# Expert weights in eight chunks instead of four, spread over the first tiles of the expert stage

## The reference

```
xn  = layernorm(x)                                     # without scale and shift
out = x + attention(xn) + ffn(xn)

attention: q = rmsnorm(xn @ W_cq), kv = rmsnorm(xn @ W_ckv); 16 heads; a head's scores are the sum of
           a 128-wide part without position and a 64-wide part with rotary position; causal softmax; W_o
ffn:       scores = sigmoid(xn @ gate_w)               # 32 experts
           the 6 largest scores of a token, divided by their sum, are its shares
           routed = sum over its 6 experts e of share * (silu(xn @ wg[e]) * (xn @ wu[e])) @ wd[e]
           shared = silu(xn @ sg) * (xn @ su) @ sd     # one expert of width 192 that all tokens use
```

## Time and profile before

| | us |
|---|---|
| three runs | 1453.88, 1455.01, 1455.03 (median 1455.01) |
| the profiled execution | 1453.54 |
| its span, from the first to the last instruction | 1451.8 |
| TensorE busy in it | 1304.7 (90%) |
| VectorE busy | 936.3 (64%) |
| ScalarE busy | 852.0 (59%) |
| GpSimd busy | 588.0 (40%) |

### The profile page before, as it was taken

The page is one execution under the profiler, slowest core; times in us unless marked ns, Lnnn a source line. Parts: engine busy times, 40 slices in busy tenths (PEclk is TensorE's granted clock), DMA queues, the critical chain, the costliest instruction groups (busy, mean ns, idle before and its releaser), DMA issues. The chain is left out here.

```text
span 1451.8 us, 24463 instructions
## 1 busy us (share of the span) xinstructions
PE 1304.7 (90%) x7385; PEld 965.7 (67%) x7385; DVE 936.3 (64%) x3727; ACT 852.0 (59%) x2294; POOL 588.0 (40%) x607
## 2 busy tenths in 40 slices
PE   4899769999998999759999999998898898998996
PEld 3566446777775777548888888875566665665664
DVE  3587678777776777313564332226888889788784
ACT  1455337677666667326566666656666666666663
POOL 1111027777776667400000000004666566566663
PEclk8999979999999999969999999999999999999998
DMA  9777552323237322286955555542232332332321
GB/s 348 302 258 258 235 200 99 109 81 109 99 113 260 103 91 77 73 260 202 336 176 175 181 177 178 177 137 80 77 106 78 108 105 81 105 103 80 104 79 55
DMA packets 132243, 216.98 MB, mean 149 GB/s; under 512 B 14550, under 2 KB 108438, under 8 KB 126870
## 3 DMA queue, kind: packets, MB, share of 16 engines
q1 hardware_dynamic: 99862, 152.48, 30.9%
q0 software_dynamic: 18432, 50.36, 10.7%
q10 hardware_dynamic: 13824, 12.59, 2.8%
HBM read 103.70 MB, written 111.67 MB: 148 GB/s over the span
## 5 line engine op out<-in xcount | busy, mean ns | idle before, releaser
L1707 ACT ACTIVATE l_prob<-l_prob,l_negmax 128x512 f32<-128x512 f32 (+3 forms) x256 | 142.1, 556 | 153.1 <-DVE l_negmax L1793 153.0
L1062 POOL DMA_INDIRECT sorted_x<-f_xn_row,slot_no x192 | 203.9, 1062 | 49.8 <-issue 49.1
L1218 ACT ACTIVATE f_prob<-f_prob,f_negmax 128x512 f32<-128x512 f32 (+3 forms) x256 | 142.6, 557 | 121.3 <-DVE f_negmax L1291 119.2
L1600 PE MATMUL ps<-l_kt,l_qt 128*128 128x512 f32 (+3 forms) x512 | 176.0, 451 | 39.0 <-DVE l_qt L1771 22.4
L1538 POOL DMA_INDIRECT l_rows<-sorted_y,slot_no x192 | 185.5, 966 | 49.2 <-issue 41.6
L2123 DVE TENSOR_TENSOR act_f<-hidden,ps 128x96 f32<-128x96 f32 x224 | 56.9, 254 | 223.7 <-ACT hidden L2098 223.0
L2060 PE MATMUL ps<-wgu_sb,xt_e 128*128 x896 | 186.1, 331 | 2.0 <-ACT xt_e L2093 2.0
L1291 DVE CUSTOM_DVE_ANT_0 f_prob<-ps,mask_add 128x512 f32<-128x512 f32 (+3 forms) x256 | 121.0, 486 | 86.4 <-issue 85.4
L1121 PE MATMUL ps<-kt_s,f_qt 128*128 128x512 f32 (+3 forms) x512 | 170.2, 447 | 5.0 <-DVE f_qt L1282 4.4
L1793 DVE CUSTOM_DVE_ANT_0 l_prob<-ps,mask_add 128x512 f32<-128x512 f32 (+3 forms) x256 | 121.9, 484 | 70.9 <-issue 69.7
L1566 POOL MEMSET l_one<- 128x1 f32 x1 | 0.1, 99 | 373.3 <-POOLq L1991 373.3
(11 more groups left out here) (202 smaller groups left out, 2955.9 us busy)
## 6 DMA issues: line engine op xcount, KB each, us to landing
sorted_x<-zeros SPq DMA_DIRECT2D x14, 2048.0 KB, 9.0
rows_in<-sorted_x SPq DMA_DIRECT2D x112, 256.0 KB, 2.9
sorted_y<-rows_out SPq DMA_DIRECT2D x112, 256.0 KB, 2.1
wgu_sb<-in_wgu SPq DMA_DIRECT2D x8, 768.0 KB, 14.0
x_in<-in_x SPq DMA_DIRECT2D x8, 512.0 KB, 9.7
xn_dram<-xn SPq DMA_DIRECT2D x8, 512.0 KB, 3.7
base_dram<-x_in SPq DMA_DIRECT2D x8, 512.0 KB, 2.9
nqt_dram<-nqt_out SPq DMA_DIRECT2D x8, 512.0 KB, 3.9
```

Source lines behind the costliest of these rows:

```text
L1062: pool.indirect_dma_start(sorted_x, bass.IndirectOffsetOnAxis(ap=slot_no[:, t, k:k + 1], axis=0), xn_row[buf][:], None).then_inc(scattered ...
L1218: act.activation(prob[:, i, qt, 0:w], prob[:, i, qt, 0:w], ACT.Exp, bias=negmax[:, i, qt:qt + 1], scale=-1.0, accum_out=rowsum[:, g // 2 % ...
L1600: mm = pe.matmul(s_ps[k % 2][:, 0:w], qt[g // 2 % 2][g % 2][:, n * P:w], kt[b - HB][:, 0:w], start=True, stop=True)
L1707: act.activation(prob[:, i, qt, 0:w], prob[:, i, qt, 0:w], ACT.Exp, bias=negmax[:, i, qt:qt + 1], scale=-1.0, accum_out=rowsum[:, g // 2 % ...
```

## The change

The weights come in eight chunks of four experts (three DMAs of 384 KB each). Two of them, as many bytes as chunk 0 had, are loaded in `heads_first`, at the same place. The other six stand in SP's list of the expert stage ahead of pairs 0, 2, 4, 6, 8 and 10. Four pairs of rows instead of three are loaded at the end of `heads_first`; so the load at pair 0 of the stage falls away. The wait for the last store of `heads_first` moves to the second iteration of the stage. As the store may now be under way while chunks arrive, `f_res` is moved out of the room into storage of its own, and `f_lat`, of the same size, takes its place in the room.

```
 class ExpertWeights:
-    CHUNKS = 4
+    CHUNKS = 8
     EACH = NE // CHUNKS
+    EARLY = 2
 ...
-            taken = size // self.CHUNKS
+            taken = self.EARLY * size // self.CHUNKS
 ...
-        for r in range(self.AHEAD - 1):
+        for r in range(self.AHEAD):
             sp.dma_start(self.rows_in[r][:], in_pairs[r]).then_inc(self.in_loaded[r], 16)
 ...
-    res = room_c.sb("f_res", [P, TT, H])
+    res = sb("f_res", [P, TT, H])
 ...
-    lat = sb("f_lat", [P, 2, S])
+    lat = room_c.sb("f_lat", [P, 2, S])
 ...
-            weights.load_chunk(sp, 0, wgu, wd)
+            for n in range(weights.EARLY):
+                weights.load_chunk(sp, n, wgu, wd)
 ...
-            sp.wait_ge(res_stored, 16 * HB + 16)
 ...
             def body(i):
                 for d in range(PAIRS):
+                    if i == 0 and d % 2 == 0 and weights.EARLY + d // 2 < weights.CHUNKS:
+                        weights.load_chunk(sp, weights.EARLY + d // 2, wgu, wd)
+                    if i == 1 and d == 0:
+                        sp.wait_ge(done.res_stored, 16 * HB + 16)
                     if i == 1:
                         last.load(sp, d, rope_dram, nqt_dram, kt_dram, nkv_dram, wq_dram, wvo_dram, done)
                     r = PAIRS * i + d
-                    if not (isinstance(i, int) and r + AHEAD - 1 >= NTILE // 2):
+                    if AHEAD <= r + AHEAD - 1 < NTILE // 2:
                         load(r + AHEAD - 1, (d + AHEAD - 1) % AHEAD)
                     if not (isinstance(i, int) and r < 2):
                         store(r - 2, d % 2)
 
-            for n in range(1, weights.CHUNKS):
-                weights.load_chunk(sp, n, wgu, wd)
             iterations(sp, body)
```

## The result

Four runs of the changed kernel took 1433.45 to 1436.87 us, median 1434.79; before, 1454.83 in the same rounds. The ratio is 0.9868 (95% interval 0.9853 to 0.9883): 20.0 us less by the medians, 17 to 21 by the interval. Predicted were 1436.6 us, and a gain of 18.45. In a later set of rounds the ratio was 0.9863 (0.9835 to 0.9892). The profiled execution took 1436.87, the slowest of the four, with a span of 1434.7; the one of the kernel before, with 1453.54, was faster than all four beside which the changed kernel was timed. So the two traces lie closer together (17.1 us by the spans) than the medians.

A forecast was written before the change was run, and what follows sets the result against it. TensorE, 90% busy, was held by a 16.5 us wait for rows queued behind early weights; 18.55 + 2.4 + 0.5 - 3.0 = 18.45 us gained gave 1436.6 us against the runs' median of 1455.01, range 1432 to 1442.

The forecast's parts named there:

- Part 1, the stall: Expert stage, tiles 5 to 8: with four pairs loaded beforehand TensorE's wait for rows goes; gain 18.55 us.
- part 3, the clock: Stage start, tiles 0 to 4: an earlier start may keep the clock high; +0.5 us taken, between -0.4 and 1.2.
- Part 2, the moved wait: End of the first heads: without SP's wait for the last store to land, TensorE starts sooner; gain 2.4 us.
- what is still in the queue is covered by the tiles ahead: Stage start: 512 KB still queued delay chunk 2 by about 1.2 us, which the tiles ahead cover.
- Part 4, the shared queue: First twelve pairs of the stage: weights and rows share the queue, so stores land late for ACT; loss 3.0 us.
- chunks 2 and 3 pass before stores flow: Early expert stage: only chunks 4 to 7 delay stores, 4 x 1.2 = 4.8 us, less 1.6 of room: 3.2 us.
- the 3 to 6 that were to show: First 28 tiles: sign that ACT's waits for `sorted_y` stores would total some 3 to 6 us.
- Small edits: Three more issues at 437, the fourth row load, chunk issues in the stage, swapped buffers: 0, at worst 0.5 us.
- The loss at the loads for the last heads: Late expert stage: the wait between 683 and 712, with 3.4 us lost before, comes again some 18 us sooner.
- Rival A: Queue in the stage: a 384 KB piece costs nearly as much as 768 KB; 28 us lost, 1461.6 us; chance 0.05.
- B: Stage up to tile 28: mixed loads, stores and weights run at 254 GB/s; loss 12 us, 1445.6; chance 0.07.
- C: End of the first heads: the block's end waits for the store anyway, moved wait brings nothing; 1439.5 us; chance 0.05.

The follow-up runs named there:

- e2: The changed kernel with SP's wait for the last store put back at the end of the first heads; 1433.9 us (one run).
- f2: The kernel of e2 again, timed in rounds beside the changed kernel: SP's wait for the last store back in its old place; 1439.3 us.
- f1: The changed kernel itself, unaltered, timed again in a later set of rounds; 1435.92 us, ratio 0.9863 to the kernel before.

## Why the prediction was right

*Part 1, the stall* (18.55) and *part 3, the clock* (+0.5), 19.05 together: tiles 0 to 8 got shorter by 31.04 - 12.17 = 18.87. Tiles 0 to 4 took 6.51 instead of 6.84 us; the granted clock was low (0.50, 1.2 GHz) at the start here too, but from 613 to 617 and not from 617 to 624. Right.

*Part 2, the moved wait* (2.4): 2.39 at the start. Wrong is the sentence that what is still in the queue is covered by the tiles ahead. The store of the heads, chunk 2 and chunk 3 are all ahead of the first store of results, and of 2.5 us some 1.0 to 1.7 were given back by the last tile. Where is not the same in the two pairs: with the wait in its old place the step to tile 8 is 2.2 instead of 4.3 us in e2, but 3.7 in both f2 and f1.

*Part 4, the shared queue* (3.0 lost): 5.4, and 5.2 in the repeat. The mechanism was the one forecast: ACT stood for stores, TensorE waited for no chunk and no rows, and two more buffers took it away. Two terms were too small. The chunk takes 4.1 us and not 3.7, since halved pieces are slower by a tenth. And "chunks 2 and 3 pass before stores flow" failed: the longest wait in the first trace, 3.2 us, is for the first store, at tile 8. With it ACT's waits come to some 10 us, not the 3 to 6 that were to show. How much each term adds is open: four chunks at 4.1 + 3.2 - 5.65 = 1.65 us, less 1.6 of room, would have been 5.0, five 6.7, and four at the old length 3.2.

*Small edits* (0): the shorter early pieces gave some 2 us in the first heads (3.3 between these two traces), where I had looked at TensorE's waits for DMAs and found none. The wait was there, one step back: TensorE waited for POOL, and POOL for a row of 128 KB on ACT's queue, which shares the engines with the chunk.

So the stall was forecast by its cause and in its size, and it is all but the whole gain. That the sum came out this near is in part luck: the last two errors cancel, 2.4 us too much lost, some 2 us not counted. The loss at the loads for the last heads came again, 18.8 us sooner (5.4 us between tiles 31 and 58, before 4.6), as forecast. Rival A lay in the right direction with a tenth of its size, B was wrong (311 GB/s in the mix; by its own numbers its loss is 11 us, not 12), and C was wrong (TensorE started 0.96 us behind the store's issue).

## What to carry to other kernels

A large transfer that nobody needs yet can be the cause of a stall when something small and urgent is issued behind it; look at what stands ahead in the queue, not at what the waiting engine names. Spreading it is not enough: its pieces must be shorter than the room of whatever is issued behind them, and the tightest room was here the store that frees a double buffer, not the load. So where a queue is made to run full, try one or two more buffers on its way out. Two were worth 4.7 us more here by the medians, and they removed a second wait that had been in the kernel all along (tiles 31 to 58 lose 2.7 to 3.1 us instead of 5.4 and 5.7).

## What the runs showed of the hardware that was not expected

- A second queue was no protection: with weights on POOL's queue and rows on SP's, the engines spent 73.1% of their time on the first and 21.0% on the second, and ACT waited up to 8.5 us for a store.
- Pieces of half the length, 3 KB a row for `wgu` and 4 KB for `wd`, moved at 287 GB/s, the whole ones at 320, with the engines full in both. Weights and rows together moved at 311 GB/s with two buffers `rows_out` and at 323 to 334 with four, again at a share of 1.0.
- A 128 KB load on ACT's queue was later beside longer pieces on SP's queue, though the bytes were the same: POOL waited 6.3 to 7.1 us for it beside 768 KB pieces (four traces), 4.7 to 5.5 beside shorter ones (ten).
- The mean granted clock at the end of the first heads was 1.00, 0.94 or 0.81, not always the same for one kernel, and the last batch took 76.3, 77.5 or 80.2 us with it.
